# Attention maxima on quarters of the TensorE array, with maxima and products in turns of two steps

## What is computed

```python
# B=4, S=1024, 16 heads of 8 numbers
scores = jnp.einsum('bhnd,bhmd->bhnm', Q, K) / jnp.sqrt(jnp.float32(D_K))
causal = jnp.tril(jnp.ones((S, S), dtype=bool))
scores = jnp.where(causal[None, None], scores, -jnp.inf)
attn = jax.nn.softmax(scores, axis=-1)
head = jnp.einsum('bhnm,bhmd->bhnd', attn, V)
```

## Time and profile before

| | us |
|---|---|
| median of 3 runs | 1017.29 |
| span of the profiled execution | 1008.0 |
| attention's prologue, maxima only | 118.0 to 148.8 |
| one quad in the middle (x = 4 to 7) | 23.85 each |
| the last quads, x = 14 and x = 15 | 27.3 and 25.6 |

### The profile page before, as it was taken

The page is one execution under the profiler, slowest core; times in us unless marked ns, Lnnn a source line. Parts: engine busy times, 40 slices in busy tenths (PEclk is TensorE's granted clock), DMA queues, the critical chain, the costliest instruction groups (busy, mean ns, idle before and its releaser), DMA issues. The chain is left out here.

```text
span 1008.0 us, 25094 instructions
## 1 busy us (share of the span) xinstructions
PE 874.2 (87%) x9373; PEld 464.7 (46%) x9374; DVE 816.2 (81%) x1699; ACT 725.7 (72%) x1493; POOL 289.1 (29%) x331
## 2 busy tenths in 40 slices
PE   4999899899999999999898898778999999979960
PEld 3666543334333333333344666533444444458850
DVE  6665499899999999999923766589999999928895
ACT  2666408788888888888784454478999999948851
POOL 4865311111111000000003656500344443005560
PEclk9999859999999999999999888768999999989995
DMA  5579851644445353330004899695354643546637
GB/s 167 223 267 331 280 133 42 205 101 105 110 98 125 89 123 84 68 69 14 13 24 127 277 317 301 226 241 101 67 118 94 114 89 54 136 142 189 206 119 252
DMA packets 121560, 147.20 MB, mean 146 GB/s; under 512 B 19213, under 2 KB 81242, under 8 KB 120800
## 3 DMA queue, kind: packets, MB, share of 16 engines
q1 hardware_dynamic: 116064, 133.74, 48.0%
q0 software_dynamic: 5376, 11.85, 4.1%
HBM read 77.63 MB, written 69.54 MB: 146 GB/s over the span
## 5 line engine op out<-in xcount | busy, mean ns | idle before, releaser
L854 ACT ACTIVATE probsB<-psB 128x512 f32<-128x512 f32 (+2 forms) x640 | 310.0, 566 | 87.1 <-PE psB L928 61.5
L766 DVE TENSOR_REDUCE mxB<-psB 128x1 f32<-128x512 f32 (+2 forms) x448 | 256.9, 642 | 11.1 <-PE psB L892 8.3
L921 PE MATMUL psB<-q_groups,k_groups 64*128 64x512 bf16 (+3 forms) x768 | 205.8, 330 | 16.6 <-DVE mxB L766 8.3
L892 PE MATMUL psB<-k_groups,q_groups 64*128 64x512 bf16 (+3 forms) x768 | 217.0, 344 | 2.8 <-PEq L293 1.7
L959 PE MATMUL psB<-probsB,vB 128*32 128x512 f32 (+3 forms) x1536 | 164.5, 500 | 0.7 <-ACT probsB L854 0.5
L1725 ACT ACTIVATE psD<-psD 128x896 f32<-128x896 f32 (+2 forms) x192 | 153.4, 799 | 12.9 <-PE psD L1779 12.7
L921 PEld LDWEIGHTS psB<-q_groups,k_groups 64*128 64x128 bf16 x768 | 67.5, 94 | 161.2 <-ACT probsB L854 140.3
L1656 DVE TENSOR_REDUCE sumsD<-psD 128x1 f32<-128x128 f32 (+3 forms) x256 | 113.2, 481 | 11.8 <-PE psD L1802 9.4
L899 PE MATMUL psB<-hideB,chooseB 64*128 64x128 bf16 (+1 forms) x1024 | 115.1, 210 | 0.0
L1779 PE MATMUL psD<-k_groups,q_groups 64*128 64x512 bf16 (+3 forms) x384 | 104.4, 343 | 12.3 <-ACT psD L1725 5.6
L766 DVE TENSOR_REDUCE mx2B<-psB 128x1 f32<-128x384 f32 (+2 forms) x192 | 104.4, 594 | 8.5 <-PE psB L899 6.9
(11 more groups left out here) (227 smaller groups left out, 1504.5 us busy)
## 6 DMA issues: line engine op xcount, KB each, us to landing
v<-vaugA SPq DMA_DIRECT2D x4, 2048.0 KB, 8.9
vB<-v SPq DMA_DIRECT2D x16, 512.0 KB
q_groups<-q SPq DMA_DIRECT2D x32, 200.0 KB
k_groups<-k SPq DMA_DIRECT2D x32, 200.0 KB
q_groups<-q SPq DMA_DIRECT2D x32, 192.0 KB
k_groups<-k SPq DMA_DIRECT2D x32, 192.0 KB
back<-emptyB POOLq DMA_DIRECT2D x16, 256.0 KB, 3.8
o<-outB SPq DMA_DIRECT2D x128, 32.0 KB, 1.8
```

Source lines behind the costliest of these rows:

```text
L766: nc.vector.tensor_reduce(dst, src, AX.X, ALU.max).then_inc(max_read, 1)
L854: nc.scalar.activation(probs[:, n % DEEP, 0:w], st[n % BANKS][:, 0:w], ACT.Exp, scale=DH ** -0.5).then_inc(exp_done, 1)
L892: ins = nc.tensor.matmul(bank[:, to:to + w], q[half[r], s, hq // 2, t * P:t * P + P], k[half[r], s, hq // 2, HALF * c:HALF * c + w], start ...
L921: ins = nc.tensor.matmul(bank[:, to:to + w], k[half[r], s, hq // 2, jt * P:jt * P + P], q[half[r], s, hq // 2, i0:i0 + w], start=True, sto ...
```

## The change

The maxima are taken over tiles of 64 queries. One unit is now a tile of 64 queries of two heads: head r of pair f = 0 or 1 goes to partitions `64 * (r ^ f)` onward of the unit's bank, so each score matmul has 64 rows and 64 columns of the array, a quarter. Two neighbouring units f = 0, 1 of the same tile use all four quarters and fill two banks. The width of a tile is rounded to 64; the four shortest tiles share a bank with a longer one (`c is None`). There are still 40 units a quad, with 17408 columns in place of 18432.

TensorE's order changes too. At each even step it issues the maxima of two units, then the products of steps e and e + 1 together (so both waits of the products, and both waits of the maxima, stand ahead of the first matmul of their pair), then a PV where one is due. `place` now issues eight DMAs of 16 pieces of 64 numbers where it issued two.

```diff
-    tiles = [(2, 0), (4, 0), (0, 0), (1, 0), (5, 0), (3, 0), (6, 1), (4, 1), (5, 1), (6, 0), (7, 0), (7, 1)]
+    kinds = [(5, 0), (13, 1), (14, 0), (2, None), (1, None), (15, 0), ...
+    def first_row(f, t):
+        return ROW_TILE * (t if ROW_TILE == 64 else 2 * t + f)
+    def max_width(f, t, c):
+        return min(HALF, first_row(f, t) + ROW_TILE - HALF * c)
+    def heads_of(f, r):
+        return [(2 * f + r, 64 * (r ^ f))] if ROW_TILE == 64 else [...]
+    def parts_of(f, t, c):
+        return [(t, 0), (t + 8, 1)] if c is None else [(t, c)]
...
                     for part in range(2):
-                        sp.dma_start(q[AUG + part:AUG + part + ROWS + 1:ROWS, x % QUADS, :, :],
-                                     neg[32 * part:32 * part + 32, x % 2, :]).then_inc(neg_placed[x % 2], 16)
+                        for f in range(2):
+                            for r in range(2):
...
+                                    sp.dma_start(dst, neg[src, x % 2, at:at + ROW_TILE]).then_inc(neg_placed[x % 2], 16)
...
                     def score(i):
-                        ins = nc.tensor.matmul(bank[:, to:to + w], q[half[r], s, hq // 2, t * P:t * P + P],
-                                               k[half[r], s, hq // 2, HALF * c:HALF * c + w], start=True, stop=(c < t // 4))
+                        for r in range(2):
+                            for hq, at in heads_of(f, r):
+                                ins = nc.tensor.matmul(bank[at:at + ROW_TILE, w * i:w * i + w],
+                                                       q[half[r], s, hq // 2, first_row(f, ti):first_row(f, ti) + ROW_TILE],
+                                                       k[half[r], s, hq // 2, HALF * ci:HALF * ci + w], start=True, stop=last)
...
+                def maxima(*both):
+                    for i in range(both[0][0]):
+                        for n, score, _ in both:
+                            if i < n:
+                                score(i)
+                        for n, _, causal in both:
+                            if causal and i < n:
+                                causal(i)
...
                     for e, (j, heads) in enumerate(steps):
-                        both = [for_products(x, e)]
-                        if todo and todo[0][1] is None:
-                            turn_over(todo.pop(0)[0])
-                        if todo:
-                            both.append(for_maximum(*todo.pop(0)))
-                        side_by_side(*both)
+                        if e % 2 == 0:
+                            if todo and todo[0][1] is None:
+                                turn_over(todo.pop(0)[0])
+                            if todo:
+                                maxima(*[for_maximum(*todo.pop(0)) for _ in range(2)])
+                            side_by_side(for_products(x, e), for_products(x, e + 1))
```

More of the change, by code:

```diff
@@ L100, in __init__ @@
         self.loaded = [m.sem(f"groups_loaded{s}") for s in range(QUADS)]
-        self.masks = [m.sb(n, [P, 2, P], BF16) for n in ("chooseB", "hideB", "hide_laterB")]
+        self.masks = [m.sb(n, shape, BF16) for n, shape in (("chooseB", [P, 2, P]), ("hideB", [P, ROW_TILE]), ("hide_laterB", [P, 2, P]))]
         self.masks_loaded = m.sem("masks_loaded")
@@ L604, in slot_width, with packs, row_tile @@
         return HALF * (c + 1) - max(HALF * c, P * jt)
-    units = [(tuple(hq ^ 1 for hq in heads), t, c) for t, c in tiles for heads in packs(max_width(t, c))]
+    def packs(w):
+        return [(0, 2), (1, 3)] if 2 * w <= HALF else [(hq,) for hq in range(4)]
+    def row_tile(f, t):
+        return 16 * f + t if ROW_TILE == 64 else 2 * t + f
+    def first_row(f, t):
[3 more added lines that the diff above has]
+    def heads_of(f, r):
+        return [(2 * f + r, 64 * (r ^ f))] if ROW_TILE == 64 else [(2 * a + r, 64 * (r ^ f) + ROW_TILE * a) for a in range(2)]
+    def parts_of(f, t, c):
+        return [(t, 0), (t + 8, 1)] if c is None else [(t, c)]
+    units = [(f, t, c) for t, c in kinds for f in range(2)]
     steps = [(j, heads) for j in range(len(slots)) for heads in packs(slot_width(j))]
-    assert [max_width(t, c) for _, t, c in units[16:] + units[:16]] == [slot_width(j) for j, _ in steps]
+    assert len(units) == len(steps)
     UNITS, SLOTS_B = len(units), len(slots)
@@ L880, in for_maximum @@
                     s = x % QUADS
-                    heads, t, c = units[g]
-                    w = max_width(t, c)
+                    f, t, c = units[g]
                     if n >= RING:
@@ L897, in causal @@
-                    def causal(i, part):
-                        r, to = heads[i] % 2, offset(heads, heads[i], w) + w
-                        ins = nc.tensor.matmul(bank[:, to - P + ROWS * part:to], choose[half[r], part, :],
-                                               hide[half[r], part, ROWS * part:P], start=False, stop=(part == 1))
-                        if part == 1 and i == len(heads) - 1:
+                        ti, ci = segments[i]
+                        w = max_width(f, ti, ci)
@@ new lines, in score @@
+                        last = first_row(f, ti) // HALF > ci
+                        for r in range(2):
+                            for hq, at in heads_of(f, r):
+                                ins = nc.tensor.matmul(bank[at:at + ROW_TILE, w * i:w * i + w],
+                                                       q[half[r], s, hq // 2, first_row(f, ti):first_row(f, ti) + ROW_TILE],
+                                                       k[half[r], s, hq // 2, HALF * ci:HALF * ci + w], start=True, stop=last)
@@ new lines, in score, with causal @@
+                        if last:
+                            ins.then_inc(max_done, 1)
+                    def causal(i):
+                        ti, ci = segments[i]
+                        to = max_width(f, ti, ci) * (i + 1)
+                        for r in range(2):
+                            at = 64 * (r ^ f)
+                            ins = nc.tensor.matmul(bank[at:at + 64, to - ROW_TILE:to], choose[half[r], 0, 0:64], hide[half[r], :],
+                                                   start=False, stop=True)
+                        if i == len(segments) - 1:
@@ L990, in _ @@
                     else:
-                        side_by_side(for_maximum(x, g))
+                        maxima(for_maximum(x, g))
                 waiting = []
@@ L2243, in constants @@
     choose = np.where(p[None, None, :] == row, 1.0, 0.0)
-    hide = np.where(p[None, None, :] > row, MASKED, 0.0)
+    hide = np.where(np.arange(ROW_TILE)[None, :] > p[:, None] % ROW_TILE, MASKED, 0.0)
     hide_later = np.where(p[None, None, :] < row, MASKED, 0.0)
```

39 lines of the change are left out of this document (19 added, 20 removed).

## The result

The changed kernel takes 1086.49 us (median of 4 runs, 1086.01 to 1091.97) against 1016.9 for the one before in the same job: ratio 1.0688, 95% interval 1.0653 to 1.0723, so slower by 69.6 us. The prediction was 1067, range 1036 to 1093.

The account below looks back on a forecast made before the run. Bound by a TensorE-ScalarE loop over three score banks, with VectorE nearly always busy. 11.6 + 15.5 = 27.1 us a quad, 49.5 us more in all: 1008.0 + 49.5 + 9.3 gave 1067, range 1036 to 1093.

Parts of the forecast that it names:

- VectorE's 1.03 us a quad are worth nothing: VectorE's reductions lose 1024 columns, 1.03 us a quad, 16.5 us for 16 quads; it now waits, so nothing is gained.
- The pair wait: In ten pairs a quad without a long PV, two steps take at least one way round with ScalarE: 11.6 us.
- ScalarE's copies stay in its gaps: ScalarE's copies in attention were to fit between its exponentials; no time was added for them.
- The order behind a PV: In ten pairs a quad behind a PV of 256 columns or more, TensorE's own row sets the time: 15.5 us.
- All four quarters at once: The maxima matmuls on all four quarters of the array run together: 0.30 us for 512 columns, 3.4 a quad.
- the rival that they run in turn: Quarters don't run at once: a pair's maxima take at least twice as long, 1.8 us more a quad, 1093; chance 0.11.
- The placing: Eight DMA issues of about 4.4 us, hidden in the prologue and in later quads: taken as 0.
- The rival of late DMAs in each quad: The eight DMAs land late and each next quad waits a microsecond or two: 20 us on top, 1085; chance 0.06.
- The last two quads: x = 14 loses 2 us through maxima in its first 24 steps, x = 15 loses 2 through waits on some pairs.
- The clock: TensorE's clock should stay granted in full.
- The sum: A middle quad takes 27.1 us against 23.85, so 45.5 over 14 quads; 49.5 with the ends; chance 0.68.
- the 9.3 us around the span: Time taken to lie outside the profiled span, added to the predicted 1057.5 us to give 1067.

## Why the prediction held, step by step

- *VectorE's 1.03 us a quad are worth nothing.* Right in this order: VectorE waits about 6 us a quad now. No run has the smaller tiles in the old order with tilings that overlap, so what they would be worth there stays open.
- *The pair wait.* The mechanism is right, and one changed wait in the kernel before is enough to show it. Its term was too small: 11.6 predicted, 12.64 measured. The hand-over from an exponential's end to the next load was taken as 0.05 us; it is 0.12 (381.70 to 381.82), since two waits stand in a row, and one wait a pair gives 0.75 back. The other 0.3 is the step "ScalarE's copies stay in its gaps", which was wrong at pair 18.
- *The order behind a PV.* The 15.5 us were right (15.65), and at 381.82 piece by piece: 0.38 to the PV, 0.99 over it, 0.29 for the maxima. Of the 4.45 us a quad 3.45 lie in the waiting pairs and 1.0 behind PVs, against 2.4 and 0.85 in my sum. That is where they lie. As causes the two can't be told apart so simply: the new order costs 2.45 even without the pair wait, and I had not said that either of them alone would make more than half of the loss.
- *All four quarters at once.* Right; 0.34 us from four of 512 columns to the next load, and the rival that they run in turn fell. In the trace a changeover is paid: from the maxima's load to the products' is 0.34 us for 512 columns (380.19 to 380.53) against 0.23 between loads of one tiling. The drain that the Trainium skill states in TensorEngine Tiling (Array Packing), section Key Properties, agrees with that. Its section Gotcha 1: PSUM Pressure, by which different row tiles can't access a bank simultaneously, is not borne out where they write different partitions of it.
- *The placing.* Taken as 0; the start costs 1.8 us more. VectorE's first copy of the maxima comes 24.1 us into attention where it came after 25.0, and the first exponential stands 9.0 us behind it where it stood 6.3. The placing is not alone in it: counted from attention's start, the first exponential comes after 31.3 us in the kernel before, 33.1 in the changed one, 33.4 in the one before with eight placings, and 32.5 on the old tiles in the new order, with two. The rival of late DMAs in each quad is true for quads of 24 us and hidden in quads of 28.
- *The last two quads.* 4 predicted, 5.8 measured.
- *The clock* stayed granted in full, as said.
- *The sum.* 49.5 predicted, 69.6 measured in attention and by the medians: 16.5 more in x = 0 to 13 (62.0 for 45.5; the middle quad gives 1.2 x 14, of it 1.05 the waiting pairs and 0.15 the others), 1.8 more in the last two, 1.8 at the start. That "the 9.3 us around the span" was a wrong reading does no harm to the 1067, which is before's median and 49.5.

## What to carry to other kernels

Before two steps are issued together, count the banks that stay in flight at the hoisted wait: with three banks and a wait for both, one exponential's way round must fit into two steps, and alone that cost 4.1 us a quad that no engine's busy time showed. A loss can have two sufficient causes, so take each out of the changed kernel as well as putting it into the old one. Relieving the busiest engine pays only if the loops next to it get no longer, so write down each loop's length (load, consumer, hand-over back) and how many steps it serves, before and after. Mends that lean on the same idle engine don't add up: measure them together.

## What the runs showed of the hardware that I had not expected

- A second wait instruction ahead of a load costs 0.07 to 0.09 us on the path: nine such pairs a quad made 0.8 us of it, and 11 us in all.
- Tiles of 64 x 128 and 64 x 64 on different halves of the rows don't overlap in any stretch looked at, at either clock (0.54 to 0.57 us a turn at 1.2 GHz, 0.31 to 0.34 at 2.4), and the kernel that alternates them was granted 1.2 GHz from its prologue to its last maxima but for 14 us; 1654.56 us in place of 1017.
- Four matmuls on quarters of the array, two of them writing each of two banks, run together: the four of 320 columns at 380.94 start within 10 ns, and their masks follow 0.16 us later.
- A row of eight small DMAs took 0.74 to 0.81 us each to issue, where a row of two took 0.55 each. Most of the eight start 0.55 to 0.8 us apart; one or two gaps of 1.2 to 1.6 in each row lift the mean.
